# Transposing two activations by DMA instead of on TensorE, in a one-core kernel of attention and a 4-bit FFN

## The chip, the cores and the metric

One Trainium2 chip, one of its cores. The metric is the device time of one launch in microseconds (us). All 16 sequences are computed in one launch.

## What is computed

The input x is 16 sequences of 512 tokens with 512 features, f32. Each sequence passes two residual sublayers; the second's weights are 4-bit codes with f16 scales for groups of 128.

```
x = x + layernorm(attention(layernorm(x)))
x = x + layernorm(ffn(layernorm(x)))

attention(h): q = h @ Wq_down.T @ Wq_up.T ; c = h @ Wkv_down.T      # rank 384 and 128
              k, v = c @ k_up[h], c @ v_up[h]                       # 16 heads of 32
              p = softmax(q k^T / sqrt(32) - slope[h] * |i - j|), causal
              return (p @ v) @ Wo.T
ffn(h):       g, u = split(h @ W_gate_up.T)                         # 2 x 1408
              y = (silu(g) * u) @ W_down.T ; return y / rms(y)
```

## The kernel before

The program runs in 17 steps, t = 0 to 16. Step t does the attention of sequence t (`att`) and the FFN of sequence t-1 (`ffn`); step 0 has no FFN, step 16 nothing else. Each engine has its own stream of instructions in a fixed order, written out by hand, and waits on semaphores.

Every large product is of f16 halves: an f32 value is held as a high half and the rest, the low half, and one product is three matmuls (high by high, high by low, low by high). In the profile these are the matmuls of L401. The operand that streams must have features on the partitions, so two activations, which are normalised with tokens on the partitions, have to be turned:

- **x**, the input of attention. DVE normalises the next sequence's tiles into `xin` in slots 48 to 51 of the step before (L855 by way of `normalise`). TensorE turns it at the head of the step: 16 transposes of 128x128 f32 against the identity (`transposes`, L407) into the PSUM banks `low0`, `low1`, `score0`, `score1`. ACT copies each bank out as the high half (`high_spare`, L692), DVE takes the rest as the low half (`low("P1", ...)`, L944). The result is `xt`, which lies over the even probability tiles.
- **x2**, the input of the FFN, is the normalised sum after attention. It is turned in the same way (L496) after two of V's four jobs: 16 transposes, four high copies, four low ones. The result is `x2t`.

The order of the work in a step on TensorE is: transposes of x; the output projection of the previous sequence (48 matmuls by `wo`); the down projection `wkv` (job C), two jobs of Q, four of K, two of Q; V's jobs 0 and 1; transposes of x2; V's jobs 2 and 3; the first 22 matmuls of the FFN; then 64 slots and their tails, each with pieces of attention (`maximum` L575, `transposed` L592, `values` L606) and a share of the FFN's 242 up and 136 down products. A PSUM bank is free for a new job when ACT (`freea`, V and WO) or DVE (`freev`, the rest) has read it.

Meanwhile DVE and ACT make z from the output projection, LayerNorm 2, the sum `x1` (L1077), LayerNorm 3's sums (L1090), and `xn2` (L855, tile `arena`), between the halves of C, Q and K. GpSimd takes the inverse roots (L1215).

SyncE issues the loads and stores: per step 24 transfers that stack the heads of Q into `qst` and 12 that stack K into `kst` (L341, L348), the rows of the log-sums (L1484), the load of the next x into `xin` (L1480), and at the end of the step for each of four tiles the store of the result and the load of the residual `x1` (L1496, L1498), when GpSimd has counted `po`.

In step 0 the weights are unpacked beside attention: 33 units, each made by GpSimd, turned by TensorE (L428), copied out as the high half by ACT (L676, for the units in `ACT_UNITS`) or by DVE (L919), the rest by DVE (L922). `UNIT_SLOT` gives each its slot. TensorE also sums a row with the matrix `ones` in slot `ROW_SLOT` (L637).

```
ACT_UNITS = [u for u in range(UNITS) if UNIT_SLOT[u] < AHEAD // 2 or UNIT_SLOT[u] > 40 and u % 2]
```

Of the kernel before, what the change touches and what calls it, by code (L numbers as in the profile page):

```python
# [16 lines left out]
B, L, D = 16, 512, 512  # L17
# [3 lines left out]
P = 128  # L21
NT = L // P
KC = D // P
HG = P // HD
NG = H // HG
# [14 lines left out]
COUNTS = {  # L40
    "dense": (0, 13, 43, 43), "freev": (0, 9, 35, 35), "freea": (0, 4, 8, 8), "spare": (0, 4, 8, 8),
    "sparefree": (0, 4, 8, 8), "hi": (0, 13, 17, 17),
    "mx": (0, 64, 64, 64), "low": (0, 64, 64, 64), "rowsum": (0, 64, 64, 64), "ln": (0, 2, 2, 2), "mh": (0, 2, 2, 2),
# [6 lines left out]
    "hl": (0, 0, 11, 11), "chain": (8, 23, 60, 52), "guess": (0, 2, 2, 2), "series": (0, 14, 14, 14),  # L50
}
# [17 lines left out]


def norm_of_y(i, nxt):

    return i + (4 if nxt and i else 3)
# [14 lines left out]

V_FIRST = 2

UNIT_SLOT = [2 * k + 1 for k in range(20)] + [41 + 3 * k // 2 for k in range(UNITS - 20)]
RING = 3

ROW_SLOT, DNORM = 4, 22

ACT_UNITS = [u for u in range(UNITS) if UNIT_SLOT[u] < AHEAD // 2 or UNIT_SLOT[u] > 40 and u % 2]

# [48 lines left out]
def layer_program(nc, x, wq_down, wq_up_t, wkv_down_t, k_up_t, v_up_t, wo_t, gu_packed, gu_scales,  # L146
# [6 lines left out]
    with ctx:  # L153
# [66 lines left out]
        steep_scale = sb("steep_scale", [P, 1], f32)  # L220
        sizes = sb("sizes", [P, 2 * MI, GROUPS], f32)
        pos_part = sb("pos_part", [P, 2 * MI, GROUPS], f32)
        rows_of = sb("rows_of", [P, 4, 2 * MI], f32)
# [3 lines left out]
        h_scale = sb("h_scale", [P, MI], f32)  # L227
        ones = sb("ones", [P, P], f32)
        down_divisor = sb("down_divisor", [P, KC], f32)
# [25 lines left out]
        def mx_bank(k):  # L255

            return spare[k % 4] if k < AHEAD else low_bank[k % 2]

        sem = {n: ctx.enter_context(nc.semaphore("s_" + n)) for n in COUNTS}
# [121 lines left out]
        def _(pe):  # L381
# [49 lines left out]
            def step(t, att, ffn, nxt):  # L431
                j = jobs(t)
                if att:

                    pe.wait_ge(sem["ln1"], val("ln1", t, 0) if not (isinstance(t, int) and t == 0) else 4)
                    for c in range(KC):
                        transposes(c, lambda i: xin[:, i, P * c:P * c + P])
# [16 lines left out]
                if att:  # L454

                    pe.wait_ge(sem["sparefree"], val("sparefree", t, 4))
                    if isinstance(t, int) and t == 0:
# [43 lines left out]
                if att:  # L501
# [3 lines left out]
                def ffn_up(m, up, a, b):  # L505

                    n = job_f(t, m, up)
                    if a == 0:
                        open_job(t, n)
                    col = I * up + P * m  # L510
                    tt = terms(lambda s, c: wgu[:, KC * s + c, col:col + P], lambda s, c: x2t[:, s, c, :], KC - 1)
                    tt += [(wgu[:, KC - 1, col:col + P], x2t[:, s, KC - 1, :]) for s in range(2)]
                    for c in range(KC if m == 0 and not up else 0):

                        pe.wait_ge(sem["sparefree"], val("sparefree", t, (4 if att else 0) + c + 1))
                        ins = products(bank(t, n)[:, :], tt[3 * c:3 * c + 3], c == 0, c == KC - 1)
                    if m or up:
                        ins = products(bank(t, n)[:, :], tt[a:b], a == 0, b == GU_PRODUCTS)
                    if b == GU_PRODUCTS:
                        ins.then_inc(sem["dense"], 1)  # L520
# [141 lines left out]
        def _(act):  # L662
# [16 lines left out]
            def step(t, att, ffn, nxt):  # L679
# [50 lines left out]

                if att:
                    for c in range(KC):
                        high_spare(c, xt[:, 0, c, :], S_X)
# [90 lines left out]
        def _(dve):  # L824
# [100 lines left out]
            def step(t, att, ffn, nxt):  # L925
# [3 lines left out]
                n_spare = [0]  # L929
                his = {"P1": 0, "C": 4, "Q": 5, "K": 7, "Q1": 11, "X2": 13 if att else 0}  # L930

                def low(kind, i, dst, scale, hi):

                    if kind in ("P1", "X2"):
# [123 lines left out]
                if isinstance(t, int) and t == 1:  # L1058
                    dve.wait_ge(s_row, 1)
                if att:  # L1060
                    for c in range(KC):
                        low("P1", c, xt[:, 1, c, :], S_X, xt[:, 0, c, :])
# [87 lines left out]
                for slot, (low_tiles, exp_tiles) in enumerate(SLOTS):  # L1150
# [307 lines left out]
        def _(sp):  # L1458
            rows = lambda a: a.rearrange("(i p) d -> p i d", p=P)

            def step(t, att, ffn, nxt):
# [25 lines left out]
                if isinstance(t, int) and t == 0:  # L1487

                    sp.wait_ge(s_blk, UNITS)
                    for i in range(NT):  # L1490
                        sp.dma_start(x1[:, i, :], x[0, P * i:P * i + P, :]).then_inc(sem["xres"], 16)
                if ffn:
# [88 lines left out]
```

## Time and profile before

| | |
|---|---|
| time, median of 3 runs | 2394.97 us (2394.91 to 2397.46) |
| the profiled execution | 2397.13 us, of it the span 2395.4 us |
| TensorE matmul busy | 2332.0 us, 97% of the span, 12830 matmuls |
| VectorE (DVE) busy | 1587.0 us, 66% |
| ScalarE (ACT) busy | 1373.2 us, 57% |
| GpSimd (POOL) busy | 684.0 us, 29% |
| mean granted TensorE clock | 0.987 |
| chain that ended last | TensorE 88%, DVE 4%, POOL 3%, ACT 2%, issue 2%, SPq 1% |

A busy engine is one that has an instruction under way; PEld is the loading of weights, which runs beside the matmuls. SPq and ACTq are the queues on which SyncE and ScalarE issue DMAs. The idle time in brackets is that of the engine just before the instruction, with what ended it. The granted clock is given as a share of 2.4 GHz. Step 8 begins at about 1279.7 us of the span; steps 1 to 15 are alike, 142.9 us each.

### The profile page before, as it was taken

Reading aid. Unit: us, or ns where it says so; the run is one execution under the profiler, and the core shown is the slowest. Engines: PE = TensorE matmul, PEld = TensorE weight load, DVE = VectorE, ACT = ScalarE, POOL = GpSimd, SP = SyncE. Lnnn points to the kernel's source line nnn. Section 1 sums busy time; section 2 is a strip of 40 time slices with the busy share of each in tenths; the row PEclk is TensorE's granted clock in tenths of the full one; section 3 lists DMA queues with packets and bytes.
Section 4 is the critical chain, followed back from the end, with each engine's and each line's share of the span. In section 5 each row is a group of like instructions: output and inputs, shape, how many; then the busy total and the mean of one; then the engine's idle time right before and its main releaser. Section 6 shows DMA issues by size and latency. Waiting matters only on the chain.

```text
span 2395.4 us, 38031 instructions
## 1 busy us (share of the span) xinstructions
PE 2332.0 (97%) x12830; PEld 1068.2 (45%) x12830; DVE 1587.0 (66%) x4407; ACT 1373.2 (57%) x3803; POOL 684.0 (29%) x948
## 2 busy tenths in 40 slices
PE   7699999999999999999999999999999999999988
PEld 3344444444444444444444444444444444444433
DVE  7867576666757667675775757666675765767543
ACT  4747466474755647466564746647475564746610
POOL 6522323122231313323132232312323131332312
PEclk9799999999999999999999999999999999999989
DMA  6020121201112130121202012120111203012000
GB/s 152 19 58 15 53 53 37 71 19 53 37 50 58 34 73 20 38 52 45 62 20 71 19 54 54 37 71 19 49 42 45 62 28 76 23 36 54 24 13 18
DMA packets 99233, 108.79 MB, mean 45 GB/s; under 512 B 22607, under 2 KB 72911, under 8 KB 99023
## 3 DMA queue, kind: packets, MB, share of 16 engines
q1 hardware_dynamic: 98174, 105.58, 16.8%
q8 instruction: 101, 1.65, 0.3%
q10 hardware_dynamic: 864, 0.79, 0.2%
q14 instruction: 94, 0.77, 0.1%
HBM read 38.42 MB, written 16.78 MB: 23 GB/s over the span
## 4 chain that ended last, share of the span: by engine, by line
PE 88%; DVE 4%; POOL 3%; ACT 2%; issue 2%; SPq 1%; DMA 0%; POOLq 0%; DVEq 0%
PE dense L401 65%; PE psO L606 6%; PE psO L401 4%; PE score L592 4%; PE low L575 3%; PE score L575 3%; DVE st_ln L844 1%; PE low L592 1%; ACT arena L790 1%; POOL rs_ln L1215 1%; PE low L407 1%; PE low L496 1%; PE score L496 1%; PE score L407 1%; POOL arena L1391 0%
## 5 line engine op out<-in xcount | busy, mean ns | idle before, releaser
L401 PE MATMUL dense<-arena,wgu 128*128 128x512 f16 x3872 | 923.4, 379 | 0.9 <-DVE arena L944 0.9
L401 PEld LDWEIGHTS dense<-arena,wgu 128*128 128x128 f16 x3872 | 375.0, 97 | 400.2 <-issue 10.6
L401 PE MATMUL dense<-wdn,arena 128*128 128x512 f16 x2048 | 517.4, 379 | 2.6 <-POOL arena L1328 2.6
L1328 POOL TENSOR_TENSOR arena<-late,arena 128x512 f16<-128x512 f32 x176 | 203.7, 1157 | 846.2 <-DVE arena L980 633.5
L1155 DVE CUSTOM_DVE_ANT_0 low<-low,mmax 128x128 f32<-128x128 f32 (+3 forms) x672 | 278.5, 435 | 211.2 <-PE low L575 209.9
L716 ACT ACTIVATE low<-low,ncol 128x128 f32<-128x128 f32 (+3 forms) x672 | 300.5, 447 | 118.2 <-DVE ncol L1155 109.7
L790 ACT ACTIVATE arena<-score 128x512 f32<-128x512 f32 (+3 forms) x672 | 280.0, 438 | 142.5 <-PE score L592 142.4
L716 ACT ACTIVATE score<-score,ncol 128x384 f32<-128x384 f32 x352 | 214.3, 609 | 142.4 <-DVE ncol L1155 142.2
L401 PEld LDWEIGHTS dense<-wdn,arena 128*128 128x128 f16 x2048 | 192.5, 98 | 180.9 <-issue 9.3
L1155 DVE CUSTOM_DVE_ANT_0 score<-score,mmax 128x384 f32<-128x384 f32 x352 | 213.8, 649 | 76.0 <-PE score L575 74.2
L1391 POOL TENSOR_SCALAR_AFFINE_SELECT arena<-arena 128x512 f32<-128x512 f32 x240 | 166.0, 692 | 248.9 <-ACT arena L790 247.6
L592 PE MATMUL score<-qst,kst 128*128 128x512 f16 (+3 forms) x784 | 217.6, 304 | 2.7 <-ACT arena L790 2.5
L606 PE MATMUL psO<-arena 128*32 128x512 f32 (+3 forms) x1920 | 178.0, 443 | 6.2 <-POOL arena L1391 4.0
L575 PE MATMUL low<-kst,qst 125*128 125x128 f16 (+3 forms) x672 | 155.2, 277 | 7.6 <-ACT low L716 7.4
L985 DVE TENSOR_SCALAR arena<-oc 128x512 f16<-128x512 f32 x64 | 28.1, 440 | 200.0 <-ACT oc L709 200.0
L957 DVE SCALAR_TENSOR_TENSOR late<-late,dense 128x512 f32<-128x512 f32 x176 | 120.6, 685 | 53.6 <-ACT late L700 53.5
L700 ACT ACTIVATE late<-dense,gate_scale 128x512 f32<-128x512 f32 x176 | 119.8, 681 | 61.0 <-PE dense L401 40.3
L790 ACT ACTIVATE arena<-low 128x384 f32<-128x384 f32 (+3 forms) x240 | 102.7, 428 | 85.4 <-PE low L592 84.7
L965 DVE SCALAR_TENSOR_TENSOR late<-late,h_scale,dense 128x512 f32<-128x512 f32 x176 | 130.9, 744 | 24.4 <-PE dense L401 24.3
L1155 DVE DVE_READ_ACCUMULATOR2_ANT ncol<- 128x1 f32 x1024 | 144.8, 141 | 0.2
L1215 POOL TENSOR_TENSOR rs_ln<-ve_ln,half 128x4 f32<-128x4 f32 x48 | 49.0, 1020 | 316.3 <-DVE ve_ln L950 311.8
L716 ACT ACTIVATION_READ_ACCUMULATOR low<-low,ncol 128x1 f32 x672 | 133.6, 199 | 0.0
(209 smaller groups left out, 2914.1 us busy)
## 6 DMA issues: line engine op xcount, KB each, us to landing
qst<-arena SPq DMA_DIRECT2D x384, 64.0 KB, 2.0
kst<-arena SPq DMA_DIRECT2D x186, 128.0 KB, 2.6
xin<-x SPq DMA_DIRECT2D x16, 1024.0 KB, 5.2
late<-x SPq DMA_DIRECT2D x64, 256.0 KB, 2.8
out<-late SPq DMA_DIRECT2D x64, 256.0 KB, 2.1
qst<-mrow SPq DMA_DIRECT2D x96, 8.0 KB, 1.9
wgu<-wo_t SPq DMA_DIRECT2D x1, 1024.0 KB, 13.1
wgu<-wq_down SPq DMA_DIRECT2D x1, 768.0 KB, 4.5
```

What stands on the lines that cost most here:

```text
L401: ins = nc.tensor.matmul(dst, w, a, start=first and k == 0, stop=last and k == len(tt) - 1)
L575: nc.tensor.matmul(mx_bank(k)[:, 0:P * (i + 1)], qst[0:P - 3, h, P * i:P * i + P], kst[0:P - 3, h, 0:P * (i + 1)], start=True, stop=True). ...
L592: ins = nc.tensor.matmul(st_bank(e)[:, 0:wide], kst[:, h, P * kt:P * kt + P], qst[:, h, P * kt:L], start=True, stop=True)
L606: ins = nc.tensor.matmul(psO[HD * a:HD * a + HD, P * kt:L], v[:, kt, HD * (HG * g + a):HD * (HG * g + a) + HD], prob_of(s)[:, a, 0:wide], ...
L700: nc.scalar.activation(tb[:, m % 2, :], bank(t, n)[:, :], ACT.Tanh, scale=gate_scale[:, m:m + 1]).then_inc(sem["tanh"], 1)
L716: nc.scalar.activation(mx_bank(k)[:, 0:wide], mx_bank(k)[:, 0:wide], ACT.Exp, scale=-1.0, bias=ncol[:, k:k + 1], accum_out=scol[:, k:k + 1 ...
L790: nc.scalar.activation(prob_of(e // HG)[:, e % HG, 0:wide], st_bank(e)[:, 0:wide], ACT.Exp, scale=1.0 / S_SCORE, **({"bias": steep_bias[:, ...
L957: nc.vector.scalar_tensor_tensor(tb[:, m % 2, :], tb[:, m % 2, :], 1.0, bank(t, n)[:, :], ALU.add, ALU.mult).then_inc(sem["freev"], 1)
L965: nc.vector.scalar_tensor_tensor(tb[:, m % 2, :], tb[:, m % 2, :], h_scale[:, m:m + 1], bank(t, n)[:, :], ALU.mult, ALU.mult).then_inc(sem ...
L1155: nc.vector.tensor_tensor_reduce(out=mx_bank(k)[:, 0:wide], in0=mx_bank(k)[:, 0:wide], in1=mmax[:, L - wide:L], scale=-1.0 / S_SCORE, scal ...
L1328: nc.gpsimd.tensor_tensor(ht[:, 1, m, :], tb[:, m % 2, :], ht[:, 0, m, :], ALU.subtract).then_inc(sem["hl"], 1)
L1391: nc.gpsimd.affine_select(out=diagonal, in_=diagonal, compare_op=ALU.is_ge, fill=0.0, base=0, pattern=[[0, HG], [1, P]], channel_multiplie ...
```

## The change

Neither x (from step 1 on) nor x2 is turned by TensorE any more. Both are split into f16 halves in token order, and each tile of 128 tokens with its two halves (1024 f16 values for a token) is turned by one DMA with `transpose=True`, 256 KB each, four for x and four for x2.

- x: after DVE has normalised a tile, it writes the two halves itself (slots 48 to 51 of the step before), into `early` for tile 0 and over `xin` for the others. SyncE issues the four transposes once `pv` shows that the even probability tiles are free, and in steps with an FFN ahead of the store of the last tile (`X_BEFORE`). TensorE waits for all four (`xt`) before job C.
- x2: ACT writes the high halves, DVE the low ones, and ACT issues the four transposes, ahead of its copies of V. TensorE waits for all four (`x2t`) before the first matmul of the FFN. V's four jobs stand together ahead of that (`V_FIRST` is 0).
- In step 0, `ones`, `sizes` and `pos_part` share the new tile `early`, `ROW_SLOT` goes from 4 to 10, and other units are copied by ACT. TensorE still turns x there.

```diff
-ROW_SLOT, DNORM = 4, 22
-ACT_UNITS = [u for u in range(UNITS) if UNIT_SLOT[u] < AHEAD // 2 or UNIT_SLOT[u] > 40 and u % 2]
+ROW_SLOT, DNORM = 10, 22
+ACT_UNITS = [u for u in range(UNITS) if u % 2 == 0 or UNIT_SLOT[u] > 40]
-V_FIRST = 2
+V_FIRST = 0
+X_BEFORE = 3
...
+        def x_halves(i):
+            return (xin[:, i - 1, :] if i else early[:, :]).bitcast(f16).rearrange("p (s d) -> p s d", s=2)
+        def x2_halves(i):
+            place = (early[:, :], oc[:, :], xn2[:, 0, :], xn2[:, 1, :])[i]
+            return place.bitcast(f16).rearrange("p (s d) -> p s d", s=2)
...
 @block.tensor
-                if att:
-                    pe.wait_ge(sem["ln1"], val("ln1", t, 0) if not (isinstance(t, int) and t == 0) else 4)
+                if isinstance(t, int) and t == 0:
+                    pe.wait_ge(sem["ln1"], 4)
                     for c in range(KC):
                         transposes(c, lambda i: xin[:, i, P * c:P * c + P])
...
-                    pe.wait_ge(sem["sparefree"], val("sparefree", t, 4))
+                    if not ffn:
+                        pe.wait_ge(sem["sparefree"], val("sparefree", t, 4))
+                    else:
+                        pe.wait_ge(sem["xt"], val("xt", t - 1, 64))
...
-                if ffn:
-                    for i in range(NT):
-                        pe.wait_ge(sem["ln3"], val("ln3", t, i + 1))
-                        for c in range(KC):
-                            ins = nc.tensor.transpose(spare[c][:, P * i:P * i + P], xn2[:, i, P * c:P * c + P],
-                                                      id32[:, :])
-                            if i == NT - 1:
-                                ins.then_inc(sem["spare"], 1)
...
+                    if m == 0 and not up and a == 0:
+                        pe.wait_ge(sem["x2t"], val("x2t", t, 64))
+                    ins = products(bank(t, n)[:, :], tt[a:b], a == 0, b == GU_PRODUCTS)
...
 @block.scalar
-                    for c in range(KC):
-                        high_spare(c, x2t[:, 0, c, :], S_X)
+                    for i in range(NT):
+                        if i < 2:
+                            act.wait_ge(sem["ln3"], val("ln3", t, i + 1))
+                        else:
+                            act.wait_ge(sem["x2l"], val("x2l", t, i - 1))
+                            act.wait_ge(sem["ln3"], val("ln3", t, i + 1))
+                        nc.scalar.activation(x2_halves(i)[:, 0, :], xn2[:, i, :], ACT.Copy, scale=S_X).then_inc(sem["x2h"], 1)
+                    for i in range(NT):
+                        act.wait_ge(sem["x2l"], val("x2l", t, i + 1))
+                        nc.scalar.dma_start(x2t.rearrange("p s c l -> p (s c) l")[:, :, P * i:P * i + P],
+                                            x2_halves(i).rearrange("p s d -> p (s d)"),
+                                            transpose=True).then_inc(sem["x2t"], 16)
...
 @block.vector
-                    for c in range(KC):
-                        low("X2", c, x2t[:, 1, c, :], S_X, x2t[:, 0, c, :])
+                    for i in range(NT):
+                        dve.wait_ge(sem["x2h"], val("x2h", t, i + 1))
+                        nc.vector.scalar_tensor_tensor(x2_halves(i)[:, 1, :], xn2[:, i, :], S_X, x2_halves(i)[:, 0, :],
+                                                       ALU.mult, ALU.subtract).then_inc(sem["x2l"], 1)
...
-                        normalise("ln1", xin[:, i, :], xin[:, i, :], i).then_inc(sem["ln1"], 1)
+                        link(t, normalise("ln1", xin[:, i, :], xin[:, i, :], i))
+                        linked(t)
...
+                        link(t, nc.vector.tensor_scalar(x_halves(i)[:, 0, :], xin[:, i, :], S_X, None, ALU.mult))
+                        linked(t)
+                        nc.vector.scalar_tensor_tensor(x_halves(i)[:, 1, :], xin[:, i, :], S_X, x_halves(i)[:, 0, :],
+                                                       ALU.mult, ALU.subtract).then_inc(sem["ln1"], 1)
...
 @block.sync
+                def x_transposed():
+                    sp.wait_ge(sem["pv"], val("pv", t, NG * NT - 1))
                     for i in range(NT):
+                        sp.wait_ge(sem["ln1"], val("ln1", t, i + 1))
+                        sp.dma_start(xt.rearrange("p s c l -> p (s c) l")[:, :, P * i:P * i + P],
+                                     x_halves(i).rearrange("p s d -> p (s d)"), transpose=True).then_inc(sem["xt"], 16)
+                if not ffn:
+                    x_transposed()
+                if ffn:
+                    for i in range(NT):
+                        if nxt and i == X_BEFORE:
+                            x_transposed()
                         sp.wait_ge(sem["po"], val("po", t, i + 1))
                         sp.dma_start(out[t - 1, P * i:P * i + P, :], stage[:, i % 2, :]).then_inc(sem[f"out{i % 2}"], 16)
```

How the order moves, at two places. On ACT, in a step with both halves, between its last copy of Q and the first rows of the softmax. Before (`oc` is a scratch tile, `arena` holds xn2, x2t, V and the halves of Q and K, `late` the FFN's working tiles):

```order
L686 ACTIVATE arena<-dense 128x512 [waits s_dense]
L764 ACTIVATE arena<-dense 128x512 [waits s_dense,s_add2]
L764 ACTIVATE arena<-dense 128x512 [waits s_dense]
L692 ACTIVATE arena<-low 128x512 [waits s_spare] x2
L692 ACTIVATE arena<-score 128x512 [waits s_spare] x2
L764 ACTIVATE arena<-psO 128x512 [waits s_dense]
L764 ACTIVATE arena<-dense 128x512 [waits s_dense]
L700 ACTIVATE late<-dense,gate_scale 128x512 [waits s_dense]
```

And now:

```order
L692 ACTIVATE arena<-dense 128x512 [waits s_dense]
L782 ACTIVATE early<-arena 128x512 [waits s_ln3,s_add2]
L782 ACTIVATE oc<-arena 128x512 [waits s_ln3]
L782 ACTIVATE arena<-arena 128x512 [waits s_ln3,s_x2l] x2
L785 DMA_TRANSPOSE arena<-early 128x8x128 [waits s_x2l]
L785 DMA_TRANSPOSE arena<-oc 128x8x128 [waits s_x2l]
L785 DMA_TRANSPOSE arena<-arena 128x8x128 [waits s_x2l] x2
L770 ACTIVATE arena<-dense 128x512 [waits s_dense] x2
L770 ACTIVATE arena<-psO 128x512 [waits s_dense]
L770 ACTIVATE arena<-dense 128x512 [waits s_dense]
L706 ACTIVATE late<-dense,gate_scale 128x512 [waits s_dense]
```

The four high copies now read `xn2` and not PSUM, the transposes stand behind them and wait for DVE's low halves, and all four copies of V stand behind the transposes.

On SyncE's queue, at the end of a step with both halves, before and now:

```order
L1496 DMA out<-late 128x512 [waits s_po]
L1498 DMA late<-x 128x512
L1496 DMA out<-late 128x512 [waits s_po]
L1498 DMA late<-x 128x512
L341 DMA qst<-arena 32x2x512 [waits s_freev]
```

```order
L1540 DMA out<-late 128x512 [waits s_po]
L1542 DMA late<-x 128x512
L1529 DMA_TRANSPOSE arena<-early 128x8x128 [waits s_ln1,s_pv]
L1529 DMA_TRANSPOSE arena<-xin 128x8x128 [waits s_ln1] x3
L1540 DMA out<-late 128x512 [waits s_po]
L1542 DMA late<-x 128x512
L356 DMA qst<-arena 32x2x512 [waits s_freev]
```

The four transposes of x stand between the third tile's store and load and the fourth's; nothing else moved there.

## Rows read from the trace of the kernel before

**Rows 1.** What TensorE waited for in one whole step (1137 to 1280 us).
```profile
PE low L592 <- DMA qst<-mrow: 0.6, 1, 0.6
```

**Rows 2.** Timeline of TensorE, end of step 7, head of step 8: start us, us, engine, line, operation.
```profile
1276.05 0.64 PE L606 MATMUL psO<-arena 128*32 128x256 f32 x8
...
1279.67 1.09 PE L407 MATMUL low<-id,xin 128*128 128x128 f32 x8
...
1281.47 5.99 PE L401 MATMUL dense<-wo,arena 128*128 128x512 f16 x27
...
1291.83 2.75 PE L401 MATMUL dense<-arena,wkv 128*128 128x512 f16 x12
```

**Rows 3.** Timeline of TensorE, from V's first jobs to the FFN, step 8.
```profile
1307.37 1.46 PE L401 MATMUL dense<-vup,ct 128*128 128x512 f16 x6
1308.66 0.38 PE L496 MATMUL low<-id,arena 128*128 128x128 f32 x2
...
1310.41 0.81 PE L401 MATMUL psO<-vup,ct 128*128 128x512 f16 x3
...
1311.82 4.91 PE L401 MATMUL dense<-arena,wgu 128*128 128x512 f16 x22
```

**Rows 4.** Timeline of DVE, the same place: xn2, the last low half of Q.
```profile
1306.29 1.91 DVE L855 TENSOR_SCALAR arena<-late,mv_ln,rs_ln 128x512 f32<-128x512 f32 x4
1308.27 0.69 DVE L944 SCALAR_TENSOR_TENSOR arena<-dense,arena 128x512 f16<-128x512 f32 x1
1310.98 1.29 DVE L944 SCALAR_TENSOR_TENSOR arena<-low,arena 128x512 f16<-128x512 f32 x2 [2.02 <-ACT arena L692]
```

**Rows 5.** Timeline of ACT, the same place: its last copy of Q.
```profile
1307.57 0.60 ACT L686 ACTIVATE arena<-dense 128x512 f16<-128x512 f32 x1 [1.99 <-PE dense L401]
```

**Rows 6.** Timeline of DVE, step 7, the first work after slots 48 to 51.
```profile
1270.31 0.43 DVE L985 TENSOR_SCALAR arena<-oc 128x512 f16<-128x512 f32 x1 [7.82 <-ACT oc L709]
1270.77 0.69 DVE L987 SCALAR_TENSOR_TENSOR arena<-oc,arena 128x512 f16<-128x512 f32 x1
```

**Rows 7.** Timeline of SyncE's queue, end of step 7 and in step 8.
```profile
1277.31 0.43 SPq L1498 DMA_DIRECT2D late<-x  x1
1286.67 0.34 SPq L1496 DMA_DIRECT2D out<-late  x1
...
1308.98 8.33 SPq L348 DMA_DIRECT2D kst<-arena  x12
```

**Rows 8.** DMA issues of the whole run: count, KB each, median us from issue to landing.
```profile
kst<-arena SPq DMA_DIRECT2D x186, 128.0 KB, 2.6
xin<-x SPq DMA_DIRECT2D x16, 1024.0 KB, 5.2
late<-x SPq DMA_DIRECT2D x64, 256.0 KB, 2.8
out<-late SPq DMA_DIRECT2D x64, 256.0 KB, 2.1
```

**Rows 9.** Windows of step 8: busy us by engine, then granted clock, DMA share, GB/s.
```profile
1276.70:1290.00 13.30, 13.30 (x76) 6.88 (x77) 6.23 (x14) 2.62 (x5) 2.60 (x4) 1.00 0.25 79
1308.60:1314.00 5.40, 5.40 (x35) 3.24 (x33) 2.84 (x5) 3.91 (x8) 0.00 (x0) 1.00 0.75 160
```

**Rows 10.** Timeline of TensorE, step 16, around its longest wait.
```profile
2298.03 0.69 PE L496 MATMUL low<-id,arena 128*128 128x128 f32 x2 [10.89 <-DVE arena L855]
...
2302.65 13.65 PE L401 MATMUL dense<-arena,wgu 128*128 128x512 f16 x52 [0.95 <-DVE arena L944]
```

**Rows 11.** Windows of step 16 around the same wait, columns as in rows 9.
```profile
2287.00:2290.00 3.00, 0.14 (x1) 0.00 (x0) 2.05 (x8) 0.72 (x2) 0.69 (x1) 1.00 0.00 0
2290.00:2298.00 8.00, 0.00 (x0) 0.00 (x0) 6.32 (x16) 0.00 (x0) 1.35 (x2) 0.51 0.00 0
...
2307.00:2308.00 1.00, 1.00 (x6) 0.37 (x5) 0.00 (x0) 0.51 (x1) 0.00 (x0) 0.86 0.00 0
```

**Rows 12.** Groups by line, step 0 (28 to 137 us): a maximum's matmul and its waits.
```profile
L575 PE MATMUL low<-kst,qst 125*128 125x128 f16 (+3 forms) x42 | 12.3, 337 | 7.6 <-ACT low L716 7.4
```

More of the change, by code:

```diff
@@ L40 @@
 COUNTS = {
-    "dense": (0, 13, 43, 43), "freev": (0, 9, 35, 35), "freea": (0, 4, 8, 8), "spare": (0, 4, 8, 8),
-    "sparefree": (0, 4, 8, 8), "hi": (0, 13, 17, 17),
+    "dense": (0, 13, 43, 43), "freev": (0, 9, 35, 35), "freea": (0, 4, 8, 8), "spare": (0, 4, 0, 0),
+    "sparefree": (0, 4, 0, 0), "hi": (0, 13, 9, 9), "xt": (0, 64, 64, 0), "x2h": (0, 0, 4, 4), "x2l": (0, 0, 4, 4), "x2t": (0, 0, 64, 64),
     "mx": (0, 64, 64, 64), "low": (0, 64, 64, 64), "rowsum": (0, 64, 64, 64), "ln": (0, 2, 2, 2), "mh": (0, 2, 2, 2),
@@ L49 @@
     "po": (0, 0, 4, 4), "out0": (16, 0, 32, 32), "out1": (16, 0, 32, 32), "tanh": (0, 0, 11, 11), "hh": (0, 0, 11, 11),
-    "hl": (0, 0, 11, 11), "chain": (8, 23, 60, 52), "guess": (0, 2, 2, 2), "series": (0, 14, 14, 14),
+    "hl": (0, 0, 11, 11), "chain": (8, 31, 68, 52), "guess": (0, 2, 2, 2), "series": (0, 14, 14, 14),
 }
@@ L220, in layer_program @@
         steep_scale = sb("steep_scale", [P, 1], f32)
-        sizes = sb("sizes", [P, 2 * MI, GROUPS], f32)
-        pos_part = sb("pos_part", [P, 2 * MI, GROUPS], f32)
+        early = sb("early", [P, D], f32)
+        ones = early[:, 0:P]
+        sizes = early[:, P:P + 2 * MI * GROUPS].rearrange("p (a b) -> p a b", b=GROUPS)
+        pos_part = early[:, P + 2 * MI * GROUPS:P + 4 * MI * GROUPS].rearrange("p (a b) -> p a b", b=GROUPS)
         rows_of = sb("rows_of", [P, 4, 2 * MI], f32)
@@ L227, in layer_program @@
         h_scale = sb("h_scale", [P, MI], f32)
-        ones = sb("ones", [P, P], f32)
         down_divisor = sb("down_divisor", [P, KC], f32)
@@ L512, in ffn_up @@
                     tt += [(wgu[:, KC - 1, col:col + P], x2t[:, s, KC - 1, :]) for s in range(2)]
[L513 to L518, printed above, removed]
+                    if m == 0 and not up and a == 0:
+                        pe.wait_ge(sem["x2t"], val("x2t", t, 64))
+                    ins = products(bank(t, n)[:, :], tt[a:b], a == 0, b == GU_PRODUCTS)
                     if b == GU_PRODUCTS:
@@ L729, in row_copy @@
                                          ).then_inc(sem["mrowc"], 1)
-                if att:
+                if not ffn:
                     for c in range(KC):
@@ L929, in step @@
                 n_spare = [0]
-                his = {"P1": 0, "C": 4, "Q": 5, "K": 7, "Q1": 11, "X2": 13 if att else 0}
+                his = {"P1": 0, "C": 4, "Q": 5, "K": 7, "Q1": 11}
+                if ffn:
+                    his = {"C": 0, "Q": 1, "K": 3, "Q1": 7}
                 def low(kind, i, dst, scale, hi):
-                    if kind in ("P1", "X2"):
+                    if kind == "P1":
                         n_spare[0] += 1
@@ L1059, in step @@
                     dve.wait_ge(s_row, 1)
-                if att:
+                if not ffn:
                     for c in range(KC):
@@ L1191, in step @@
                         dve.wait_ge(sem["rs"], val("rs", t, norm_of_x(ffn)))
-                        normalise("ln1", xin[:, i, :], xin[:, i, :], i).then_inc(sem["ln1"], 1)
+                        link(t, normalise("ln1", xin[:, i, :], xin[:, i, :], i))
+                        linked(t)
+                        if i:
+                            dve.wait_ge(sem["ln1"], val("ln1", t, i))
+                        elif ffn:
+                            dve.wait_ge(sem["xt"], val("xt", t - 1, 64))
+                        else:
+                            dve.wait_ge(s_row, 1)
+                        link(t, nc.vector.tensor_scalar(x_halves(i)[:, 0, :], xin[:, i, :], S_X, None, ALU.mult))
+                        linked(t)
+                        nc.vector.scalar_tensor_tensor(x_halves(i)[:, 1, :], xin[:, i, :], S_X, x_halves(i)[:, 0, :],
+                                                       ALU.mult, ALU.subtract).then_inc(sem["ln1"], 1)
                 o_split(NG - 1)
@@ L1491, in step @@
                         sp.dma_start(x1[:, i, :], x[0, P * i:P * i + P, :]).then_inc(sem["xres"], 16)
+                def x_transposed():
[4 more added lines that the diff above has]
+                                     x_halves(i).rearrange("p s d -> p (s d)"), transpose=True).then_inc(sem["xt"], 16)
+                if not ffn:
+                    x_transposed()
                 if ffn:
                     for i in range(NT):
+                        if nxt and i == X_BEFORE:
+                            x_transposed()
                         sp.wait_ge(sem["po"], val("po", t, i + 1))
```

## The prediction

> **What bounds the kernel now.** I read the page first, then the waits of one whole step, then the timeline of each engine where the transposes stand. TensorE waits 0.6 us in a step of 142.9 us [rows 1]: it is the bound in steps 1 to 15, and whatever leaves its stream is won, provided nothing new makes it wait. So there are two questions: how much leaves, and whether the data that now come by DMA are there when TensorE arrives.
>
> **What leaves TensorE.** x: the first transpose starts at 1279.67, the output projection behind it at 1281.47: 1.80 us a step, 15 steps [rows 2]. x2: from 1308.66 to 1310.41, 1.75 us [rows 3], 16 steps. If all of it were won the run would be 55 us shorter, some 2.3%.
>
> **x, new path.** DVE gets two more passes for each of four tiles, one like L985 (0.43 us) and one like L987 (0.69) [rows 6]: 4.5 us. They fall in slots 48 to 51, behind which DVE idled 7.82 us [rows 6]; cost nothing while that holds. The tenants of the idle time, LayerNorm of y and its store, come up to 4 us later, and their readers are the store queue, not TensorE. The ACT and DVE copies out of PSUM at the step's head go; they were beside the output projection and win nothing. SyncE reaches the transposes at about 1277.7, after the third tile's load [rows 7]; the last even probability tile has been read by then (1276.69) [rows 2]. TensorE needs xt at job C, 1291.83 before [rows 2], 1290.0 now. That leaves 12.3 us for four transfers of 256 KB. Behind them on the queue stand only the fourth tile's store, which came at 1286.67 [rows 7], and its load.
>
> **x2, new path.** I keep the clock of the old trace and take the 1.8 us of x off at the end, since the chain from the output projection to xn2 hangs on TensorE and moves with it. xn2 is complete at 1308.20, the low half of Q's last job at 1308.96 [rows 4]; ACT is done with Q at 1308.17 [rows 5]. Then four high passes on ACT (0.60 each at most) and four low ones on DVE, 0.61 to 0.69 apart [rows 4, 5]; tiles 2 and 3 overwrite places that the lows of tiles 0 and 1 have read, so the engines alternate. ACT has its fourth high at about 1310.8 and can issue; the last low ends at about 1311.5. TensorE runs V's four jobs meanwhile and stands at 1310.0 (1311.82 less the transposes' 1.75). Before, it never stood here. From now on it waits for the last of four transposes.
>
> **Their price, G, from the first issue to the last landing.** No row shows a transposing DMA. From below: plain stores of 256 KB, 0.34 us apart, land 2.1 us after issue [rows 7, 8]; the last can be issued at 1311.5 and lands at 1313.6, so G is 2.8. Next, one plain load of the same 1 MB: 5.2 us [rows 8]. From above: each of the 32 blocks of 128x128 as dear as one plain issue of the queue, 0.34 to 0.69 us (8.33 for 12) [rows 7]: 11 or 22, with landing 13 to 24. I take **9**. The stacks of Q and K use the same DMA engines just here: share 0.75 at 160 GB/s, so 213 GB/s when full [rows 9]. 1 MB at that rate takes 4.9 us alone and 9.8 when the stacks take turns with it; with a landing of 2, that is 6.9 to 11.8, and the first two transposes can run ahead of the last low. For x, where these stacks don't run, the same gives about 7, well inside 12.3.
>
> The Trainium skill speaks for the low side: Advanced Engine Details and Errata, X-Bar Transpose (TRN2), says transposing DMAs are as fast as plain ones, at 350 to 400 GB/s. By that 1 MB is 3 us plus the landing (an estimate), and the sum would be some 2,460; no run here shows it yet.
>
> **The clock.** In step 16 TensorE stood 10.89 us [rows 10]. The granted clock was 1.00 over 2287 to 2290, 0.51 over 2290 to 2298, and came back in 2307 to 2308 (0.86) [rows 11], so 4.4 us after the FFN began at 2302.65 [rows 10], with matmuls at 1.2 instead of 2.4 GHz: half of that, 2.2 us, was lost. A stand of 8.8 us in each step (1310.0 to 1318.8, shorter by what follows) should do the same. Bounds: 0 where the stand is short, 4.5 if the whole 9 us from 2298.03 counted. I take 2.2.
>
> **The sum for a step.** x2t lands at 1310.8 + 9 = 1319.8, less 1.8 is 1318.0; before, the FFN began at 1311.82 [rows 3]. That is +6.2, with the clock +8.4; 15 steps, +126. **Step 16** has no V jobs and no stacks: lows follow the last normalise (2299.35, from 2297.43) and end at 2301.8, transposes at 7 from about 2300.8 land at 2307.8, against 2302.65: +5; the clock is low there anyway. **Step 0**: five units' high copies leave ACT where ACT's softmax rows hold TensorE up [rows 12], 3.0 us at most; eleven leave DVE later, 7.6 at most; DVE gets 4.5 for the halves of x. Between -10 and +5, I take -3. Sum: 2397.1 + 126 + 5 - 3 = 2525, against the profiled execution's 2397.1. The median of the runs is 2 us below that execution, so 2523.
>
> **Rivals.**
> 1. *Transposes as quick as the quickest plain store* (G 2.8, clock holds). The FFN begins at 1313.6 - 1.8 = 1311.8, as before; 0 a step, +1 in step 16, -3 to -10 in step 0: 2395 down to 2388, thus no change or faster. It decides for this if the last lands within 2.1 us of the last low half. For it: TensorE would stand only 3.6 us. Against: the stacks in rows 9, and the 2.6 us of the stacks themselves [rows 8]. 0.12, half for each sign.
> 2. *As a plain load of 1 MB* (G 5.2): x2t at 1316.0 - 1.8 = 1314.2, +2.4, clock +2.2: 15 x 4.6 = 69, +2, -3: 2465. At G 4 with the clock held, 2415. 0.25.
> 3. *Block by block* (G 13 to 24). Queue and transfer take the 32 blocks one after another. At 16: x2 +13.2, clock +2.2; x lands at 1293.7, 3.7 late; 19.1 a step, 287, +12, -3: 2691. At 13, 2600; at 18, 2750. ACT's copies of V stand behind the issues, but they are done before x2t lands. The fourth tile's store and residual load slip with them. 0.20.
> 4. *Far slower still*, above 24: 0.05.
>
> To rival 3 and 4 the skill has a figure: VectorE: DVE Perf Modes, The three transpose paths, gives 1309 ns for one 128x128 block by DMA, against 390 on TensorE. If 32 of them came in a row G would be 42 us and the run some 3,500 (an estimate); if they overlap over the DMA engines it says nothing against G of 9. The trace has no such row.
>
> **How the numbers follow.** Forecast (G 7 to 12) 0.38, rivals 0.12, 0.25, 0.20, 0.05. About 0.2% (5 us) is what a measurement of this kernel tells from no change. Faster 0.06, same 0.06, slower 0.88. The range 2410 to 2760 leaves out rival 1, rival 4 and the end of rival 3, 0.20 together.
>
> **What would show it.** L407 gone after step 0, L496 gone. Matmuls 12830 less 240 and less 256. A wait of TensorE at the first matmul by `wgu` in each step, put down to a DMA from `early`, `oc` or `arena`, of some 8 to 9 us; the granted clock at 0.5 for some us after it; none before the matmul by `wkv`. A step of about 151 us instead of 142.9. Wrong if the transposes land within 3 us, or if TensorE also waits at `wkv`.

## The result, and the profile after

The changed kernel takes 2700.51 us (median of 4 runs, 2689.47 to 2704.18) against 2394.94: a ratio of 1.1266, 95% interval 1.1232 to 1.13. It is 306 us slower. The forecast was slower by 128, so the sign held and the size was 2.4 times too small.

The page of the profiled execution (2704.18 us, span 2702.4). First the busy times and the clock in 40 slices, then two groups by line, with busy time, mean ns, and the idle time ahead of them:

```profile
PE 2346.6 (87%) x12334; PEld 1027.3 (38%) x12334; DVE 1647.9 (61%) x4461; ACT 1347.0 (50%) x3749; POOL 688.8 (25%) x948
...
PEclk8889989898998989989898998989989898998989
...
L416 PE MATMUL dense<-arena,wgu 128*128 128x512 f16 x3872 | 961.2, 391 | 246.5 <-DMA arena<-arena 246.5
...
L612 PE MATMUL psO<-arena 128*32 128x512 f32 (+3 forms) x1920 | 182.3, 453 | 59.4 <-POOL arena L1422 57.5
```

TensorE has 496 matmuls fewer, as the change says, and is no longer busy throughout. It now waits in two places: 246.5 us for a DMA ahead of the FFN's first product, and 57.5 us for GpSimd's causal mask ahead of `values`; before, the only wait in a step was 0.6 us [rows 1]. The granted clock, 0.987 in the mean before, is 0.929, and falls in every step.

The first wait, in the timeline of TensorE in step 8 (start, us, operation), to be laid beside [rows 2, 3]:

```profile
1281.25 6.00 PE L416 MATMUL dense<-wo,arena 128*128 128x512 f16 x27
...
1291.62 2.75 PE L416 MATMUL dense<-arena,wkv 128*128 128x512 f16 x12
...
1309.10 0.81 PE L416 MATMUL dense<-vup,ct 128*128 128x512 f16 x3
1325.13 7.79 PE L416 MATMUL dense<-arena,wgu 128*128 128x512 f16 x22 [15.22 <-DMA arena<-arena]
```

And the timeline of ACT at that place, its last high copies and the four transposes, then V's copies:

```profile
1309.38 1.23 ACT L782 ACTIVATE arena<-arena 128x512 f16<-128x512 f32 x2 [0.39 <-DVE early L1151]
1309.99 1.39 ACTq L785 DMA_TRANSPOSE arena<-early  x1
1311.42 2.77 ACTq L785 DMA_TRANSPOSE arena<-oc  x1
1314.23 4.72 ACTq L785 DMA_TRANSPOSE arena<-arena  x2
1318.99 1.09 ACT L770 ACTIVATE arena<-dense 128x512 f32<-128x512 f32 x2 [8.38 <-issue]
```

From the first issue at 1309.99 to TensorE's start at 1325.13 are 15.1 us: that is G, for which the forecast took 9. Issuing alone takes ACT 8.9 us. Job C, at 1291.62, does not wait: x's transposes are in time.

In step 16, where no stacks of Q and K are moved, the same four cost 7.5 us (2602.13 to 2609.60). The queue of ACT, then TensorE:

```profile
2602.13 1.25 ACTq L785 DMA_TRANSPOSE arena<-early  x1
2603.41 1.35 ACTq L785 DMA_TRANSPOSE arena<-oc  x1
2604.80 2.75 ACTq L785 DMA_TRANSPOSE arena<-arena  x2
```

```profile
2609.60 30.58 PE L416 MATMUL dense<-arena,wgu 128*128 128x512 f16 x130 [20.91 <-DMA arena<-arena]
```

In step 8 both sides suffer. The stacks of K, 2.6 us before [rows 8], now land after 6.2. From the DMA issues, with median us from issue to landing:

```profile
kst<-arena SPq DMA_DIRECT2D x186, 128.0 KB, 6.2
...
arena<-xin SPq DMA_TRANSPOSE x45, 3.3
...
arena<-arena ACTq DMA_TRANSPOSE x32, 8.1
```

These are medians of the whole run. The last three of x's transposes, at the end of a step where no stacks are moved, land after 3.3 us, x2's third and fourth after 8.1. The windows of step 8 (columns as in rows 9) show the DMA engines full (the share adds up the queues' packets and can pass 1) and the clock at its lower level, 1.2 GHz, from 1314 until after the FFN has begun:

```profile
1312.00:1314.00 2.00, 0.00 (x0) 0.00 (x0) 0.00 (x0) 0.00 (x0) 0.00 (x0) 0.98 1.13 213
1314.00:1316.00 2.00, 0.00 (x0) 0.00 (x0) 0.00 (x0) 0.00 (x0) 0.00 (x0) 0.50 1.20 172
...
1328.00:1330.00 2.00, 2.00 (x6) 0.73 (x5) 0.00 (x0) 0.00 (x0) 0.00 (x0) 0.50 0.50 110
1330.00:1332.00 2.00, 2.00 (x8) 0.78 (x7) 0.69 (x1) 0.69 (x1) 0.00 (x0) 0.75 0.00 0
```

The whole of G as one window:

```profile
1309.99:1325.13 15.14, 0.00 (x0) 0.03 (x1) 1.29 (x2) 2.69 (x6) 0.00 (x0) 0.63 1.14 169
```

169 GB/s over 15.14 us are 2.56 MB, of which x2's four transposes are 1.05. K's twelve stacks, 1.57 MB, are issued in the same time (1309.08 to 1321.24 on SyncE's queue), so nearly all of them must be the rest.

The FFN's first 22 matmuls take 7.79 us there, 4.91 before [rows 3].

The second wait, which the forecast did not have, in three timelines at the end of step 7. DVE:

```profile
1252.33 1.37 DVE L1220 TENSOR_SCALAR early<-xin 128x512 f16<-128x512 f32 x1
1253.74 1.00 DVE L1222 SCALAR_TENSOR_TENSOR early<-xin,early 128x512 f16<-128x512 f32 x1
...
1256.74 0.43 DVE L1220 TENSOR_SCALAR xin<-xin 128x512 f16<-128x512 f32 x1
...
1261.13 0.55 DVE L1073 TENSOR_SCALAR late<-late,rs_lo,ve_lo 128x512 f32<-128x512 f32 x1
...
1262.17 1.37 DVE L1220 TENSOR_SCALAR xin<-xin 128x512 f16<-128x512 f32 x1
```

GpSimd:

```profile
1257.09 0.63 POOL L1422 TENSOR_SCALAR_AFFINE_SELECT arena<-arena 128x512 f32<-128x512 f32 x1
1261.77 1.49 POOL L1365 TENSOR_TENSOR late<-late 128x512 f32<-128x512 f32 x1 [4.05 <-DVE late L1073]
1263.21 1.85 POOL L1422 TENSOR_SCALAR_AFFINE_SELECT arena<-arena 128x512 f32<-128x512 f32 x2
```

TensorE:

```profile
1264.08 1.08 PE L612 MATMUL psO<-arena 128*32 128x256 f32 x8 [3.83 <-POOL arena L1422]
1265.10 1.03 PE L598 MATMUL score<-qst,kst 128*128 128x512 f16 x2
1265.92 1.91 PE L416 MATMUL dense<-wdn,arena 128*128 128x512 f16 x4
```

DVE's new passes stand ahead of `y_norm(1)` (L1073), which ends at 1261.7. GpSimd has stood 4.05 us at the add that needs it (`y_add`, L1365), and the next two causal masks (L1422) are behind that add in its order. TensorE waits 3.83 us for the first of them, and four products then take 1.91 us instead of 1.03: the granted clock is 0.50 from 1264 to 1268 and 1.00 again from 1270.

**Where a step's time goes.** The 142.9 us that the text ahead of the prediction gives for every step is one of the longer ones. In the mean a step was 142.45 us ((2276.60 - 139.89) / 15, from the head of step 1 to that of step 16) and is 162.42 ((2578.15 - 141.92) / 15): +19.97. Of it:

| | us a step |
|---|---|
| transposes off TensorE | -3.55 |
| wait for x2t, (246.5 - 20.9) / 15 | +15.04 |
| the first 22 products, mean 7.42 instead of 4.91 | +2.51 |
| wait for the mask, (57.5 - 2.5) / 15 | +3.67 |
| the rest, by difference (the clock after the wait for the mask, above all, by e3) | +2.30 |

15 such steps are 299.5; step 0 adds 2.0 (its end moved from 139.89 to 141.92), step 16 5.4 (the FFN begins 31.45 us after the step's head, 26.05 before).

### The profile page after: what moved, and what is told of

It reads as the page before. It is cut to its first block, busy times and chain, and to the rows that moved or that the text cites. A ratio compares the mean times of both kernels' runs of the same rounds, so it can differ in the third digit from the quotient of the medians.

```text
span 2702.4 us, 37147 instructions
## 1 busy us (share of the span) xinstructions
PE 2346.6 (87%) x12334; PEld 1027.3 (38%) x12334; DVE 1647.9 (61%) x4461; ACT 1347.0 (50%) x3749; POOL 688.8 (25%) x948
## 4 chain that ended last, share of the span: by engine, by line
PE 71%; DVE 14%; DMA 5%; ACTq 3%; ACT 3%; issue 3%; POOL 1%; DVEq 0%; POOLq 0%; SPq 0%
PE dense L416 54%; DMA arena<-arena 5%; PE psO L612 4%; PE psO L416 3%; PE score L598 3%; PE low L581 3%; ACTq L785 3%; PE score L581 2%; DVE st_ln L860 1%; DVE xin L871 1%; DVE arena L871 1%; DVE arena L962 1%; DVE xin L1222 1%; DVE arena L1151 1%; POOL late L1365 1%
## 5 line engine op out<-in xcount | busy, mean ns | idle before, releaser
L416 PE MATMUL dense<-arena,wgu 128*128 128x512 f16 x3872 | 961.2, 391 | 246.5 <-DMA arena<-arena 246.5
L416 PEld LDWEIGHTS dense<-arena,wgu 128*128 128x128 f16 x3872 | 384.0, 99 | 675.7 <-issue 307.7
L416 PE MATMUL dense<-wdn,arena 128*128 128x512 f16 x2048 | 534.3, 388 | 2.6 <-POOL arena L1359 2.6
L1422 POOL TENSOR_SCALAR_AFFINE_SELECT arena<-arena 128x512 f32<-128x512 f32 x240 | 171.8, 718 | 264.7 <-ACT arena L806 264.7
L612 PE MATMUL psO<-arena 128*32 128x512 f32 (+3 forms) x1920 | 182.3, 453 | 59.4 <-POOL arena L1422 57.5
L598 PE MATMUL score<-qst,kst 128*128 128x512 f16 (+3 forms) x784 | 226.9, 317 | 2.2 <-ACT arena L806 2.1
L416 PE MATMUL dense<-wo,arena 128*128 128x512 f16 x576 | 129.7, 379 | 0.0
```

The lines of the kernel that those rows point to most:

```text
L416: ins = nc.tensor.matmul(dst, w, a, start=first and k == 0, stop=last and k == len(tt) - 1)
L598: ins = nc.tensor.matmul(st_bank(e)[:, 0:wide], kst[:, h, P * kt:P * kt + P], qst[:, h, P * kt:L], start=True, stop=True)
L612: ins = nc.tensor.matmul(psO[HD * a:HD * a + HD, P * kt:L], v[:, kt, HD * (HG * g + a):HD * (HG * g + a) + HD], prob_of(s)[:, a, 0:wide], ...
L1422: nc.gpsimd.affine_select(out=diagonal, in_=diagonal, compare_op=ALU.is_ge, fill=0.0, base=0, pattern=[[0, HG], [1, P]], channel_multiplie ...
```

## The experiments

The theory after this reading: (a) x2's transposes are late because ACT issues them one after another and because the stacks of Q and K share the DMA engines; (b) x's transposes are on time, but DVE's splitting delays GpSimd's masks through `y_norm` and `y_add`; (c) each stand costs again in the clock.

**e1: x by DMA alone.** x2 is turned by TensorE again.

```diff
-V_FIRST = 0
+V_FIRST = 2
...
+                if ffn:
+                    for i in range(NT):
+                        pe.wait_ge(sem["ln3"], val("ln3", t, i + 1))
+                        for c in range(KC):
+                            ins = nc.tensor.transpose(spare[c][:, P * i:P * i + P], xn2[:, i, P * c:P * c + P],
+                                                      id32[:, :])
```

> The changed kernel with x2 turned by TensorE again (two of V's jobs ahead of it), x still by DMA; all of the output is computed. Theory: the new wait of 3.7 us a step on values <- POOL (with the clock that falls after it, some 2 us) belongs to x's part, because DVE's extra passes in slots 48 to 51 make y_norm(1) late, GpSimd stands at y_add(1) and its next causal masks come late. Then 1.8 us a step are won and 5.7 lost: 2395 + 15 x 3.9 = about 2453. Rival: the wait is a consequence of x2's stall, and x's part alone wins its 1.8 us: 2395 - 27 = 2368, and no wait of TensorE on POOL but the 4.0 us of before.

Measured: 2450.0 us, ratio 1.0222 (1.0206 to 1.0237), +53. What TensorE waited for in the whole run (total us, times, longest):

```profile
PE psO L624 <- POOL arena L1422: 58.9, 29, 3.8
```

The wait for the mask is there without x2's change, so it is x's. The rival falls.

**e2: x2 by DMA alone.** x is turned by TensorE again, and DVE does not split it.

```diff
-                if isinstance(t, int) and t == 0:
-                    pe.wait_ge(sem["ln1"], 4)
+                if att:
+                    pe.wait_ge(sem["ln1"], val("ln1", t, 0) if not (isinstance(t, int) and t == 0) else 4)
                     for c in range(KC):
                         transposes(c, lambda i: xin[:, i, P * c:P * c + P])
...
-                        if nxt and i == X_BEFORE:
-                            x_transposed()
```

> The changed kernel with x turned by TensorE again, x2 by DMA; all of the output is computed. Theory: the wait at the first matmul by wgu is all of x2's part: 15 us a step, the clock 2.9, less 1.75 won: +16.2 a step, +5 in step 16: 2395 + 243 + 5 = about 2643, and the wait on POOL of 57.5 us is gone. Rival: the wait on POOL stays (57 us), then about 2700. The two differences of e1 and e2 should add to the whole, 306.

Measured: 2630.55 us, ratio 1.0975 (1.0958 to 1.0991), +233; the two waits are

```profile
PE dense L416 <- DMA arena<-arena: 247.7, 16, 20.8
...
PE psO L609 <- POOL arena L1406: 3.8, 4, 2.5
```

So the two waits belong to the two parts. Their costs add to 286, not 306. In e2 the first 22 products after the wait take 6.99 us in the mean, in the changed kernel 7.42, which is 6 of the 20 us. A step of e1 is 145.91 us ((2330.35 - 141.71) / 15); without its wait for the mask, 3.76 us, and the 1.80 won, 1.50 us are left by difference, against 2.30 in the changed kernel: 12 us more. Either stand costs more clock when the other is there too; why is not shown.

**e3: x split four slots later.**

```diff
-LN1_SLOT, LN1_POWER, LN1_NORM = 45, 47, 48
+LN1_SLOT, LN1_POWER, LN1_NORM = 45, 47, 52
```

> The changed kernel with the normalising and splitting of the next x four slots later (LN1_NORM 52 instead of 48), so behind y_norm(1) and in DVE's idle 7 us; nothing else. Theory: the wait on POOL goes, and with it the clock's fall there: 15 x 5.7 less, about 2615. Rival: it was the number of DVE's passes and not their place: the wait only moves to a later value step, 2680 to 2710.

Measured: three of the four runs took 2607.25 to 2616.72 us, the fourth 8374.76 for a reason that is not known. The median of the three is 2609.98 (2613.35 with the fourth), 91 less than the changed kernel; ratio to the kernel before 1.0898 (1.0873 to 1.0922). The wait for the mask fell from 57.5 us to

```profile
PE psO L612 <- POOL arena L1422: 3.6, 4, 2.2
```

The same passes, behind `y_norm(1)`, make no wait any more. It was their place. 91 / 15 = 6.0 us a step, of which (57.5 - 3.6) / 15 = 3.6 were the wait, so 2.4 came after it, in line with the 2.30 by difference.

**e4: e1 and e3 together**, so x alone by DMA, split in slots 52 to 55.

> e1 and e3 together: x by DMA, split four slots later, x2 by TensorE; all of the output is computed. If the theory of e1 and e3 is right nothing waits any more and x's 1.8 us a step are won: 2395 - 27 = 2368, ratio 0.989, faster than both kernels. Rival: the transposes of x land too late or slow the stacks: a wait at the first matmul by wkv, 2395 or more.

Measured: 2367.91 us, ratio 0.9882 (0.9867 to 0.9896): **faster than both kernels, than the one before by 1.2%**. TensorE waits for nothing in steps 8 and 9 (its list of waits for 1170 to 1450 us is empty), and steps follow each other 1.80 us sooner, which are exactly the 16 transposes; from its timeline of TensorE, two steps in a row:

```profile
1155.95 4.91 PE L416 MATMUL dense<-arena,wgu 128*128 128x512 f16 x22
```

```profile
1296.56 4.91 PE L416 MATMUL dense<-arena,wgu 128*128 128x512 f16 x22
```

1296.56 - 1155.95 = 140.61; in the kernel before, a step that is not the longer one is 142.41 (1168.88 - 1026.47).

**e5: the stacks behind x2t.**

```diff
+                    if ffn:
+                        sp.wait_ge(sem["x2t"], val("x2t", t, 64))
                     taken(sp, t, j["K"] + NG - 1)
```

> The changed kernel, in which SyncE issues K's stacks and Q's second ones only when x2t has landed, so that the four transposes of x2 have the DMA engines to themselves. Theory (contention): the wait at the first matmul by wgu falls from 15.0 to 7.5 to 8 us a step, since in step 16, without stacks, the last transpose landed 7.5 us after the first issue against 15.1 in step 8. Rival (the queue: ACT issues them one after another, at the same pace whatever else runs): 13 us or more stay. The whole time tells little here, since the stacks then come too late for the first maxima: a new wait low <- kst of about 6 us a step.

Measured (one run): 2570.24 us, 130 less than the changed kernel. Queue of ACT and timeline of TensorE in one step, then the landing times of the whole run:

```profile
1248.31 1.25 ACTq L785 DMA_TRANSPOSE arena<-early  x1
1249.60 1.35 ACTq L785 DMA_TRANSPOSE arena<-oc  x1
1250.99 2.75 ACTq L785 DMA_TRANSPOSE arena<-arena  x2
```

```profile
1255.81 6.23 PE L416 MATMUL dense<-arena,wgu 128*128 128x512 f16 x22 [7.58 <-DMA arena<-arena]
```

```profile
kst<-arena SPq DMA_DIRECT2D x186, 128.0 KB, 2.6
...
arena<-arena ACTq DMA_TRANSPOSE x32, 3.3
```

G is 7.5 us (1248.31 to 1255.81) instead of 15.1, as in step 16: half of it was the stacks. In the other half two things take nearly the same time, the four issues in a row, 5.4 us, and the moving of 1 MB; e6 and e8 take them apart. The part of the expectation on the stacks was wrong: no wait on `kst` appears, and the whole run gained. The first maximum comes some 6 us after the FFN begins and the stacks of the first head are there.

**e6: plain copies in place of x2's transposes**, same tiles, rows of 256 bytes; x2 stays in token order, so what follows is computed on it unturned.

```diff
-                                            x2_halves(i).rearrange("p s d -> p (s d)"),
-                                            transpose=True).then_inc(sem["x2t"], 16)
+                                            x2_halves(i).rearrange("p s (c l) -> p (s c) l", c=KC)
+                                            ).then_inc(sem["x2t"], 16)
```

> The changed kernel with x2's four transposing DMAs replaced by plain copies of the same bytes between the same tiles, in rows of 256 bytes (x2 is then not turned: the FFN's input is left in the wrong order). Theory: the price is the moving of 1 MB in rows of 256 bytes beside the stacks, and turning adds little: the wait at wgu stays at 13 to 15 us. Rival: turning itself is dear: the wait falls to 8 us or less, the issue from 1.3 us to about 0.35 to 0.6, and the whole time by 15 x 7 = 105 us or more.

Measured (one run): 2642.36 us. From its waits of TensorE, and its issues on ACT's queue by line (ns, least, median, most):

```profile
PE dense L416 <- DMA arena<-arena: 191.1, 16, 20.1
```

```profile
L785 ACTq DMA_DIRECT2D arena<-arena x32: 743/1619/2152, 172.1 to 2543.0; - x32
L785 ACTq DMA_DIRECT2D arena<-early x16: 602/616/677, 170.6 to 2540.9; - x16
```

The wait is (191.1 - 20.1) / 15 = 11.4 us a step, between the two expectations. Turning costs 3.6 us of the 15.0; three quarters of the wait would be there for a plain copy in such rows. The first issue is half as long (0.62 against 1.29 us), but that is not where the time goes: in step 16, where no stacks are moved, the four issues take 3.3 us instead of 5.4 and the wait is only 0.8 shorter (20.1 against 20.9). The DMA engines are full there, in e6 (first line) and in the changed kernel (second):

```profile
2544.00:2545.00 1.00, 0.00 (x0) 0.00 (x0) 0.00 (x0) 0.00 (x0) 0.00 (x0) 0.50 1.03 222
```

```profile
2606.00:2607.00 1.00, 0.00 (x0) 0.00 (x0) 0.00 (x0) 0.00 (x0) 0.00 (x0) 0.50 0.99 193
```

**e8: high halves alone**, four transposes of 128 KB; the FFN reads the high half twice, and the low one is left out.

```diff
...
-                        nc.scalar.dma_start(x2t.rearrange("p s c l -> p (s c) l")[:, :, P * i:P * i + P],
-                                            x2_halves(i).rearrange("p s d -> p (s d)"),
+                        nc.scalar.dma_start(x2t[:, 0, :, P * i:P * i + P],
+                                            x2_halves(i)[:, 0, :],
```

> The changed kernel with x2's transposes cut to the high half: four of 128 KB and 4 blocks each instead of four of 256 KB and 8 blocks; the FFN takes the high half twice in place of the low one (x2's low half is left out). Theory (price by bytes and blocks): issue 0.7 instead of 1.3 us, the wait at wgu half of 15, 7 to 9 us. Rival (a price per DMA): issue 1.3 us, the wait stays at 13 or more.

Measured (one run): 2635.8 us, the wait (187.4 - 20.0) / 15 = 11.2 us a step.

```profile
L785 ACTq DMA_TRANSPOSE arena<-early x16: 1207/1222/1407, 171.0 to 2534.2; - x16
```

Half the bytes and blocks, and the first issue is as long (1.22 against 1.29 us): on ACT's queue the price is one per DMA, not one per block. The wait lies between the two expectations. In step 16 it hardly moved (20.0 against 20.9), though the engines were no longer full (share 0.30 to 0.66 from 2535 to 2540): there the issues, 5.2 us, and the last landing held it. So G without stacks is held by the issues (e8) and, as far as plain copies in such rows can tell, by the moving (e6), and easing either alone gives less than 1 us. What shrank in steps 1 to 15 is the moving beside the stacks.

**e7 and e9: matmuls in the gap.** 60 more matmuls in each step while x2t is awaited, their result unread. In e7 they stand behind the FFN's `open_job`, in e9 ahead of it. The edit of e9:

```diff
+                    if m == 0 and not up and a == 0 and "V" in j:
+                        for k in range(60):
+                            nc.tensor.matmul(low_bank[0][:, :], wkv[:, 0, 0, :], wo[:, 0, 0, :], start=True, stop=True)
                     if a == 0:
                         open_job(t, n)
```

> The changed kernel with 60 more matmuls on each step's TensorE stream (128x512 f16 into a bank that nobody reads then) ahead of the wait for x2t: 13 us of work inside a wait of 15. Theory: the clock then doesn't fall there; the wait shrinks to 2 us, nothing else moves, and the first 22 products of the FFN take 4.9 us and not 7.8: 15 x 2.9 = 44 us less, about 2657. Rival: the clock costs nothing that isn't hidden: 2700.

Measured: 2819.77 us, ratio 1.1754 (1.173 to 1.1778), 119 slower than the changed kernel. The place was wrong, and tells something:

```profile
PE low L524 <- ACT arena L773: 142.7, 15, 9.8
```

`open_job` waits for ACT's copy of V, which stands behind the transposes on ACT: 9.5 us a step of stand even before the 13 us of filling. So even if x2t had landed sooner, the FFN could not have begun until ACT had issued all four.

> As e7, with the 60 matmuls ahead of the FFN's open_job, so also ahead of the wait for ACT's copy of V, which stands behind the transposes on ACT. Theory: 13 us of the 15 are then filled, the wait for x2t shrinks to 2 us, the clock doesn't fall there, and the first 22 products take 4.9 us: 15 x 2.9 = 44 us less than the changed kernel, about 2657. Rival: the fallen clock cost nothing: 2700.

Measured: 2675.86 us, ratio 1.1163 (1.1137 to 1.1188), 25 less than the changed kernel, 44 expected. TensorE's timeline in step 8:

```profile
1296.67 13.11 PE L518 MATMUL low<-wo,wkv 128*128 128x512 f16 x60
1311.85 4.91 PE L416 MATMUL dense<-arena,wgu 128*128 128x512 f16 x22 [2.07 <-DMA arena<-arena]
```

With TensorE at work the clock stays at 2.4 GHz here (granted 1.00 from 1296 to 1318) and the first 22 take 4.91 us in 13 of 15 steps (6.6 in two, so 5.14 in the mean against 7.42: 34 us in all); the rest of the gap, 13.11 + 2.41, is 0.5 us longer than the 15.04 of the changed kernel, which takes 7 back. 44 was too high since I had put step 8's 2.9 for the mean of 2.5. The clock was a cost of its own.

**e10: e3 and e5 together**: both inputs by DMA, x split later, stacks behind x2t.

> e3 and e5 together: x's split four slots later, and K's stacks and Q's second ones behind x2t; x and x2 both by DMA, all of the output is computed. Theory: the two causes are apart and add: 2700 - 87 - 130 = about 2483; the wait left is 7.5 us a step at the first matmul by wgu. It stays slower than before, since 7.5 us and the clock are more than the 3.55 us that leave TensorE. Rival: the stacks, late as they are, then hold up the maxima: 2500 or more.

Measured: 2494.17 us, ratio 1.041 (1.0394 to 1.0425), 206 less than the changed kernel where 217 was expected from the parts. The two causes are apart to within 11 us, which stay open (15 if e3 is taken at 91). What is left is the wait of 7.5 us:

```profile
1216.80 6.38 PE L416 MATMUL dense<-arena,wgu 128*128 128x512 f16 x22 [7.47 <-DMA arena<-arena]
```

## Why the prediction was right and wrong

The direction was right; two steps of the working failed, each worth about half of the error: DVE's new passes were put at nothing, and G was taken at 9 us. In order of the prediction:

- **TensorE bounds the kernel, and what leaves it is won if nothing waits: right.** e4 wins 1.80 us a step, to the hundredth.
- **x by DMA is in time: right.** Its first issue is at 1279.41 and not 1277.7, which the room of 12.3 us took up. No wait ahead of job C in step 8 or in the waits of the whole run.
- **DVE's new passes "cost nothing while that holds": wrong.** The step that failed is "their readers are the store queue, not TensorE". I followed DVE's idle time and `y_norm`'s own result, but not GpSimd's order: `y_add` stands ahead of the causal masks, which TensorE needs. 6.0 us a step, 91 in all (e3). I had also priced the passes at 0.43 and 0.69 us, and some took 1.37 and 1.00.
- **x2's chain up to the first issue: right, to 0.6 us.** On the forecast's clock, which has the output projection at 1281.47, it had the first issue at 1310.8 and TensorE at the end of V's jobs at 1310.0. Here the projection begins at 1281.25; with the 0.22 added the first issue is at 1310.2 and TensorE at 1310.1.
- **G = 9: the mis-sized term.** The case alone was well sized (7 against 7.5, though it left out the second bound, 5.4 us of issues and a landing). Beside the stacks it was 15.1. I let the transposes and the stacks take turns, which is 2.1 MB at 213 GB/s in 9.8 us. In the trace 2.56 MB pass before the last transpose has landed, since nearly all of K's stacks go in the same time, and they pass at 169 GB/s. Against the 9.8 us, by these figures (an estimate), the bytes are 2.2 us and the rate 3.1. The plain copies of e6 are slow beside the stacks too, so turning is the smaller part. The sum held a wait of 9.8 (1310.0 to 1319.8; the 8.8 in the paragraph on the clock is a slip that did not enter it). It is 15.04: 5.2 a step, 79 us of the error. G itself was 6.1 too small, in part made up by that earlier issue.
- **The clock: right in kind and size.** 2.2 forecast, 2.51 at the FFN; but the second stand brought another 2.3. Rows 11 give 4.6 us at the lower level and not 4.4 (0.86 over 2307 to 2308 is 0.28 us at half), which makes the 2.2 a 2.3.
- **Steps 16 and 0.** +5 forecast, +5.4 measured; -3 forecast, +2.0 measured, inside its bounds.
- The error of 178 us (306 less 128) is these terms: 79 for G, 90 for the wait behind GpSimd with its clock (5.97 a step), 5 for the clock at the FFN, 5 for step 0.
- **Rival 3** at G 16 gave 2691, close to the 2700, but with other terms: its queue priced by the block, where e8 shows a price per DMA, and its 3.7 us for x, which did not come; 6.0 for DVE's place stood in their stead. Its total was right by chance.

The Trainium skill's rule, that transposing DMAs are as fast as plain ones (Advanced Engine Details and Errata, X-Bar Transpose (TRN2)), is nearly borne out here for the moving, but not for the whole. With the DMA engines to themselves in step 16 the transposes move 179 to 197 GB/s while all four are under way, with their issues holding them back too, the plain copies of e6 210 to 222; the page's 350 to 400 GB/s is reached by neither. x's transposes land after 3.3 us where a plain store of the same size takes 2.0 and a plain load 2.8, and the issue is twice that of the plain copy in e6. The 1309 ns for one block (VectorE: DVE Perf Modes, The three transpose paths) are not paid per block: eight blocks in one DMA land after 3.3 us.

## What to carry to other kernels

Before work is added to an engine's idle time, follow every reader of what it delays, and on each reader's engine what stands behind the reader; here a late add on GpSimd held up a mask that had nothing to do with it. A transfer moved onto the critical path has to be priced at the rate it gets beside the transfers that are there at that moment, with its issue times in a row on its own queue, and what stands behind them on that engine. Of two similar edits, try each alone: here one wins 1.2% once its place is right, and the other loses in every form that was tried.

## What the runs showed that I had not expected

- The first transposing DMA of a group keeps ACT's queue for 1.22 to 1.29 us whether it carries 4 or 8 blocks of 128x128 (e8, e5), against 0.62 us for a plain copy in rows of 256 bytes (e6) and 0.34 on SyncE's for a store in rows of 2 KB [rows 7]. The later ones take 1.35 each in e5, and up to 3.76 beside the stacks in the changed kernel.
- Holding the stacks of K and the second ones of Q back until x2t had landed made no new wait and gave back 130 us (e5): the stacks had been issued earlier than they were needed.
- DVE's copy to halves (L1220) takes 0.43 us in some tiles and 1.37 in others; in the rows above the long one at 1262.17 runs while GpSimd's add (L1365) is under way. No run here shows that the one causes the other.
